# First attention round prepared inside the embedding stage: projection, rotation, K pages and V gathers between the embedded groups

## What is computed

```python
W = weights[condition]                                   # (64, 32, 32): one of 16 mixing matrices per sequence
y = einsum('bct,bcd->bdt', x, W)                         # mixes the 32 tokens
x = x + (y.astype(f16) @ dequantise(qweight, qzeros, scales) + bias)
# attention: 32 query heads, 8 key/value heads of width 128, 512 cached keys in 16 pages of 32, and 32 new keys
q, k, v = x @ Wq.T, x @ Wk.T, x @ Wv.T
q, k = rope(rmsnorm(q, q_norm_w), pos), rope(rmsnorm(k, k_norm_w), pos)   # pos = cache_seqlens + arange(32)
k_all, v_all = concat(k_cache[block_table], k), concat(v_cache[block_table], v)
out = softmax(mask(q @ k_all.T * SCALE)) @ v_all @ Wo.T
```

## Time and profile before

| | |
|---|---|
| median of 3 runs | 3275.6 us (3273.37 to 3278.69) |
| the profiled execution | 3281.08 us, span in the profile 3279.6 us |
| TensorE busy | 3045.8 us (93%), granted clock 0.971 on average |
| VectorE, ScalarE, POOL busy | 1544.9, 1289.2, 1557.0 us |
| DMA | 378.97 MB, mean 116 GB/s |
| first instruction of the embedded groups on TensorE | 36.53 us |
| attention block entered | 127.2 us |
| first scores of round 0 | 178.15 us |

### The profile page before, as it was taken

The page is one execution under the profiler, slowest core; times in us unless marked ns, Lnnn a source line. Parts: engine busy times, 40 slices in busy tenths (PEclk is TensorE's granted clock), DMA queues, the critical chain, the costliest instruction groups (busy, mean ns, idle before and its releaser), DMA issues. The chain is left out here.

```text
span 3279.6 us, 56025 instructions
## 1 busy us (share of the span) xinstructions
PE 3045.8 (93%) x15264; PEld 2027.5 (62%) x15264; DVE 1544.9 (47%) x3914; ACT 1289.2 (39%) x3015; POOL 1557.0 (47%) x1335
## 2 busy tenths in 40 slices
PE   3689999999999999999999999999999996888887
PEld 2356666666666666666666666666666663555454
DVE  4334444444444444444444444444444444556555
ACT  1244444444444444444444444444444431222121
POOL 8455555555555555555555555555555520000000
PEclk9889999999999999999999999999999997999898
DMA  6724444444444443535334444344444343112110
GB/s 220 261 59 131 121 127 123 123 117 123 123 121 122 119 119 116 193 116 167 116 116 119 125 122 122 117 119 120 120 125 127 117 156 104 31 37 50 34 30 13
DMA packets 416381, 378.97 MB, mean 116 GB/s; under 512 B 83460, under 2 KB 347796, under 8 KB 415157
## 3 DMA queue, kind: packets, MB, share of 16 engines
q1 hardware_dynamic: 364676, 200.64, 20.9%
q0 software_dynamic: 50640, 174.92, 17.1%
q10 hardware_dynamic: 864, 0.63, 0.1%
HBM read 341.75 MB, written 25.85 MB: 112 GB/s over the span
## 5 line engine op out<-in xcount | busy, mean ns | idle before, releaser
L537 DVE CUSTOM_DVE_ANT_0 ps_s<-ps_s,mask 128x544 f32<-128x544 f32 x512 | 375.0, 732 | 950.6 <-PE ps_s L360 798.8
L319 PE MATMUL ps_t<-wqkv,xT 128*128 128x512 f32 x1536 | 724.2, 595 | 7.1 <-DMA xT<-x1T_scratch 7.1
L212 POOL DMA_INDIRECT v_sb<-in_v_rows_w,v_row x512 | 497.3, 971 | 477.4 <-PE ps_oT L385 264.1
L383 PEld LDWEIGHTS ps_oT<-pT,v_sb 128*128 128x128 f32 x4096 | 528.0, 192 | 184.6 <-issue 183.9
L435 ACT ACTIVATE ps_s<-ps_s,nmax 128x544 f32<-128x544 f32 x512 | 352.3, 688 | 606.3 <-DVE nmax L537 518.3
L383 PE MATMUL ps_oT<-pT,v_sb 128*128 128x128 f32 x4096 | 542.5, 276 | 7.4 <-issue 7.3
L343 PE MATMUL ps_t<-wo,oT 128*128 128x512 f32 x1024 | 524.7, 596 | 3.5 <-ACT v_raw L430 1.4
L359 PE MATMUL ps_s<-k_sb,qT 128*128 128x416 f32 x1024 | 448.8, 520 | 15.2 <-issue 11.0
L547 DVE TENSOR_SCALAR p_sb<-ps_s,rinv 128x544 f32<-128x544 f32 x512 | 401.4, 784 | 23.5
L450 ACT ACTIVATE oT<-ps_oT 128x128 f32<-128x128 f32 x512 | 142.6, 278 | 656.4 <-PE ps_oT L385 610.1
L319 PEld LDWEIGHTS ps_t<-wqkv,xT 128*128 128x128 f32 x1536 | 264.5, 192 | 198.0 <-issue 190.7
(11 more groups left out here) (212 smaller groups left out, 3757.5 us busy)
## 6 DMA issues: line engine op xcount, KB each, us to landing
k_sb<-in_kT SPq DMA_DIRECT2D x2048, 64.0 KB
xT<-x1T_scratch POOLq DMA_DIRECT2D x32, 256.0 KB
tab<-rope_scratch POOLq DMA_DIRECT2D x32, 256.0 KB
v_sb<-in_v_rows_w,v_row POOLq DMA_INDIRECT x512
wo<-in_wo_w POOLq DMA_DIRECT2D x2, 4096.0 KB, 14.3
v_new<-v_raw SPq DMA_DIRECT2D x128, 64.0 KB, 1.9
y_scratch<-y_sb SPq DMA_DIRECT2D x32, 256.0 KB
wqkv<-in_wqkv_w SPq DMA_DIRECT2D x6, 1024.0 KB, 12.7
```

The source lines that it names most:

```text
L212: e.indirect_dma_start(out=v_sb[:, b % 2, c, :], out_offset=None, in_=A["v_rows_w"], in_offset=bass.IndirectOffsetOnAxis(ap=v_row[:, b, c: ...
L319: m = e.matmul(ps_t[bank_of(t)][:, :], xT[:, k, :], wqkv[:, k, 512 * t:512 * t + 512], start=k == 0, stop=k == KC - 1)
L383: e.matmul(ps_oT[:, :], v_sb[:, b % 2, c, h * D:(h + 1) * D], pT[:, u % 2, c, :], start=c == 0, stop=False)
L537: e.tensor_tensor_reduce(out=scores(u), in0=scores(u), in1=mask[:, b % 2, :], scale=-SCALE, scalar=3e38, op0=ALU.add, op1=ALU.min, accum_o ...
```

## The change

The tiles and semaphores that both stages need (`raw`, `rot`, `tab`, `xT`, `k_sb`, `v_sb`, ...) are made once, in a class `Shared` whose object `W` lives through both stages. `embed` places its short-lived tiles (packed weights, angles, sines, gathered mixing matrices) inside them. `rotate` becomes a function of the module; its text is the same. What changes in the order of work:

- The mixing matrices come in three parts (groups 0 to 3, 4 to 9, 10 to 15). TensorE waits only for the part that it needs.
- The angles are computed by VectorE, three of their steps as one fused instruction each, ahead of the dequantisation. The table with the minus sign is no longer computed: the norm weights are negated instead.
- The loads for the fold and all six loads of `wqkv` are issued by ScalarE, ahead of its first copy of a group. ScalarE also issues the stores of x1T.
- In groups 4 to 9 TensorE, ScalarE and VectorE also handle one projection tile of round 0 each. x1T of group 0 is written straight into `xT`.
- SP loads K pages of the first two sequences, four after each of groups 5 to 12.
- POOL makes the tables in two halves through one half-size buffer, takes those of group 0 by a copy, then issues the first eight V gathers and runs both rotations of round 0.
- The two sums of the fold are done by VectorE after groups 10 and 12. All 16 groups are written out, no loops.
- The load of the first half of `wo` is issued at the start of the attention, where TensorE now begins with `turn_q`.

```diff
@@ attention @@
-            e.dma_start(xT[:, :, :], x1T_d[0]).then_inc(dma_x, 16)
-            e.dma_start(tab[:, :, :], tab_d[0]).then_inc(dma_tab, 16)
...
-            load_v(0, 0)
-            load_v(0, 1)
+            load_x(1)
             e.dma_start(wo[:, :, :], A["wo_w"][0]).then_inc(dma_wo[0], 16)
-            rotate(0, 0)
-            rotate(0, 1)
-            e.wait_ge(raw_copied, NT)
-            load_x(1)
             body(0, 2)
...
-            for t in range(NT):
-                project(0, t, 0, KC)
             for t in range(NQT):
                 turn_q(0, t)
             score(0, 0, 0)
@@ embed @@
+    MIX_PARTS = [(0, 4), (4, 10), (10, GROUPS)]
+    SPREAD_AT = {1: 1, 5: 2}
+
+    FOLD_AT = 3
+    PROJECT_AT = {4: 0, 5: 1, 6: 2, 7: 3, 8: 4, 9: 5}
+    PAGES_AT = {5: (0, 0), 6: (0, 1), 7: (0, 2), 8: (0, 3), 9: (1, 0), 10: (1, 1), 11: (1, 2), 12: (1, 3)}
+    SUMS_AT = {10: ("w2f", "w2"), 12: ("b2f", "b2")}
...
+            # gpsimd
+            gather(0)
+            gather(1)
...
+            tables(0)
+            gather(2)
+            e.wait_ge(out_tab, 16)
+            tables(2)
...
+            e.wait_ge(deq, 1)
+            for b in range(2):
+                for c in range(LC):
+                    e.indirect_dma_start(out=W.v_sb[:, b, c, :], out_offset=None, in_=A["v_rows_w"],
+                                         in_offset=bass.IndirectOffsetOnAxis(ap=W.v_row[:, b, c:c + 1], axis=0)).then_inc(W.dma_v[b], 16)
...
+            rotate(e, W, 0, 0)
+            rotate(e, W, 0, 1)
...
+            # tensor
+            def project(t):
+
+                if t == 0:
+                    e.wait_ge(x1T_copied, 1)
+                    e.wait_ge(folded_a, 2)
+                e.wait_ge(dma_wqkv[t], 16)
+                wait(e, W.summed, t - 1)
+                for k in range(KC):
+                    m = e.matmul(ps_p[bank_of(t)][:, :], W.xT[:, k, :], wqkv[:, k, 512 * t:512 * t + 512], start=k == 0, stop=k == KC - 1)
+                m.then_inc(W.projected, 1)
...
+            # scalar
+            e.wait_ge(dma_q, 16 * 5)
+            for name in ("w2t", "b2t", "a13", "w2", "b2"):
+                e.dma_start(fold[name], A["c_" + name]).then_inc(dma_fold, 16)
+            e.wait_ge(ang_ready, 1)
+            e.activation(sn, ang, ACT.Sin).then_inc(trig, 1)
+            e.activation(cs, ang, ACT.Sin, scale=0.5).then_inc(trig, 1)
+            for t in range(NT):
+                at = slice(512 * t, 512 * t + 512)
+                e.dma_start(wqkv[:, :, at], A["wqkv_w"][0][:, :, at]).then_inc(dma_wqkv[t], 16)
...
+                wait(e, out_xT[g % 2], 16 * (g // 2))
+                e.activation(to, ps_x[g % 2][:, :, :], ACT.Copy).then_inc(x1T_copied, 1)
+                e.wait_ge(x1T_copied, g + 1)
+                e.dma_start(x1T_d[g], to).then_inc(out_xT[g % 2], 16)
```

More of the change, by code:

```diff
@@ L885, in body @@
[L885 removed]
+            spread(0)
+            e.wait_ge(W.dma_bt, 16)
+            e.tensor_scalar(W.bt[:, :], W.bt[:, :], 0, PAGES - 1, ALU.max, ALU.min).then_inc(W.bt_bounded, 1)
+            for g in range(GROUPS):
+                i = g % 2
                 e.wait_ge(ffn_done, g + 1)
```

486 lines of the change are left out of this document (251 added, 235 removed).

## The result

| | before | after |
|---|---|---|
| median, same chip | 3277.14 us (4 runs) | 3244.91 us (3236.72 to 3248.76, 4 runs) |
| profiled execution, its span | 3281.08, 3279.6 us | 3248.76, 3246.8 us |
| first mix on TensorE | 36.53 us | 39.88 us |
| attention entered | 127.2 us | 133.6 us |
| first scores of round 0 | 178.15 us | 143.50 us |

The ratio is 0.9897, with a 95% interval of 0.9885 to 0.991. The change gains 32 us where 53 were predicted, and the time lies above the range of 3207 to 3238. The first scores came at 143.5, not at 125: these 18.5 us are nearly all of the 20.8 us between the profiled execution and the 3228 predicted for it.

What follows compares the result with a forecast made beforehand. TensorE fills the rounds, so the first score's time decides. Lead-in -40.6 and earlier block entry -12.5 sum to -53 us: 3281.1 to 3228 for the profiled execution, 3222 for the median; range 3207 to 3238.

Steps and rivals of the forecast that it cites:

- Lead-in: From block entry to first scores of round 0: falls from 50.9 to 10.3 us, -40.6 us, leaving mainly `turn_q`.
- The rounds keep what the start gains: Rounds after the first are untouched, so what the first score gains, the whole gains: 53 us.
- rival D: Rounds stay at clock 0.94 instead of 1.00 after the denser start: 116 us slower, 3392; chance 0.03.
- Start of the groups: Before the first groups: angles on VectorE 7.5 us, first `mix` at 25 to 31 us instead of 36.5.
- The port cost: POOL's second tables blocking VectorE in groups 4 or 5: counted as 2 us, range 0 to 8.
- Standing in issue until about 32: ScalarE's queue at the start: issuing fold and `wqkv` loads delays its first copy to 32 us, range 26 to 40.
- The stall at group 2 to 3: Third x1T copy waits for a store queued behind eleven loads on ScalarE's queue, until 50 us.
- The fold's product on TensorE hides in this stall: At groups 2 to 3: the fold's product runs during the stall that lasts until 50 us, so it costs nothing extra.
- Groups 4 to 9: Each takes 2.51 us plus a projection tile of 3.81 us, 6.32 us; from 51 to 90 us.
- Groups 10 to 15: Late groups to last cast: 12.6 us plus 3 for fold sums, with pages and port conflicts; last cast at 107.6.
- Last cast to entry: End of the embedding to attention entry: 7.1 us as before, so the block is entered at 114.7 us.
- Rival B: Transfers or POOL set the end of the groups: gain 42 or 43 us, 3234 or 3233; chance 0.20.

Runs made afterwards that it cites:

- fold_first: Changed kernel with the fold's product and its copies moved ahead of the first mix on TensorE; 3230.91 us, ratio 0.9853.
- start_rebuilt: Changed kernel with the edits of tables_wait and fold_first, POOL waiting for each table product, and VectorE's fold sums after groups 2 and 3; 3231.08 us, ratio 0.9848.
- spread_first: Changed kernel with VectorE spreading the first part of the mixing matrices before the angles; 3234.55 us, ratio 0.9861.
- tables_wait: Changed kernel with the first spread between angles and dequantisation, and POOL's tables waiting for the dequantised weight; 3237.45 us, ratio 0.9865.
- same_again: Changed kernel run once more, unaltered; 3239.01 us, ratio 0.9871.

## Why the prediction was right and wrong

*Lead-in*, -40.6 us: right. From block entry at 133.64 to the first scores there are 9.9 us, against 10.3 predicted and 50.9 before. `turn_q` ran at 1.86 us a tile directly behind entry.

*The rounds keep what the start gains*: right on the whole. That 3103.3 and 3101.5 us agree within 2 us is luck in part, since other kernels with the same rounds took 3091.0 to 3109.6. The clock in the stretch from 290 on is 1.00 again, so rival D fell.

*Start of the groups*: "First `mix` at 25 to 31" came at 39.88. The angles (15.37 to 23.4, 8 us) cost what was said, 7.5. The failed terms are "the spread of four groups about a quarter of 4.32 us", which measured 8.08, and the last step of the dequantisation, 2.80 for 1.23 us. Both stand beside POOL's work on the tables, which starts as soon as ScalarE has its sines. The port cost was counted once, for the second tables, at 2 us of a range of 0 to 8. Measured are about 8.4 us at the first tables (6.8 and 1.6) and 8.4 at the second (9.13 for 0.69). This is the first step that failed: a cost put at nothing in one place and at 2 us in the other. The prediction had priced the whole run, 10 us, and took it for the upper end.

*"Standing in issue until about 32"*: the issues ended at 29.46, within the 26 to 40 given. But the first copy, set to 32 by it, came at 42.00, because it waited for TensorE.

*"The stall at group 2 to 3"*, until 50: wrong in mechanism, near in time. No copy waited for the x1T store. A transfer did hold TensorE until 53.90, but it was the x tile of group 4 on SP's queue, 18 us behind the last issue of the weights. That POOL's first table store filled the engines then fits the times, but was not tried. What held group 4 longer was VectorE's addition, to 61.68.

*"The fold's product on TensorE hides in this stall"*: wrong, the second step that failed. TensorE did stand idle, for 4.22 and 4.58 us, but both times ahead of the fold: in its order the fold comes behind the transpose of group 2, which needs the long addition. So the 8.1 us stand bare behind it; fold_first got 7.5 us back. Together the steps put the end of the fold at 70.7 where group 4 was to start at 51, 19.7 us late. Groups 4 to 9 won back 3.4 and groups 10 to 15 lost 2.7, which leaves 19.0 at the last cast and 18.5 at the first scores.

Repairs do not recover all of it: with both collisions and the fold out of the way start_rebuilt cast group 4 at 57.75, and the earliest first scores of any run are 131.04, not 125.

*Groups 4 to 9* at 6.32 us each: they took 5.63, a little better. *Groups 10 to 15* with pages and sums: 20.3 us against 17.6, with two waits for x tiles of 3.13 and 2.60 us in them. *Last cast to entry*, 7.1: measured 7.0. *POOL* ended its rotation near 120 instead of 102, before the block ended at 133.6, so off the path as said.

*Rival B*, transfers or POOL set the end: in the changed kernel only in small, by these two waits and the x tile at 53.90. It became the limit when the other losses were gone, and then through the pages on SP's queue, not as a sum of bytes at a rate.

The size of the gain was overstated because each mechanism that I could name was priced by its own row, and the one that the trace before showed clearly, 9.97 us for one addition, was discounted to 2.

## What to carry to other kernels

When two engines block each other, the same instruction can lose one instruction of the other engine or a whole run of them. So price the collision by the longest row of it, at every place where the moved work can meet the other engine, and not once. When work moves into a stage, look at what it makes earlier: a gain on one engine slides the loads behind it into the transfers of another queue, and single gains of 7 us need not add up. Before work is to hide in a stall, look on which side of the stall its place in the order is. Keep bulk loads off the queue of the load that the next step needs.

## What the runs showed of the hardware that was not expected

**VectorE can wait out a whole run of POOL products.** Beside four products of 2.3 us back to back one addition that takes 0.42 or 0.69 us alone took 9.97 (the kernel before), 9.13, 8.90, 8.98, 8.98 and 10.93 us in six kernels. In spread_first and tables_wait no addition beside such a run took more than 2.73 us, about one product. The four small copies lost about one product each, never a run. With a wait of POOL behind each product no addition beside the tables took more than 2.73.

**TensorE pauses where the hardware loop of the rounds returns, in some executions and not in others.** The timeline of TensorE in the changed kernel at such a place, and the table by stretch around it:

```profile
784.29 1.13 PE L359 MATMUL ps_s<-k_sb,qT 128*128 128x416 f32 x2 [2.03 <-issue]
783.00:789.00 6.00, 4.71 (x11) 2.43 (x12) 0.79 (x2) 1.06 (x4) 3.77 (x4) 0.72 0.68 201
```

It waits for nothing that the profile shows for 2.03 us, then some us at the lower clock (0.72 on average over these 6 us). At the same place of fold_first there is no pause:

```profile
782.65 0.86 PE L359 MATMUL ps_s<-k_sb,qT 128*128 128x416 f32 x2
```

Such pauses of over 0.5 us between 230 and 1300 us, about 159 us or a multiple of it apart, one turn of a loop of two rounds, were six in the changed kernel, five of them in this rhythm (10.4 us), two in same_again (4.2), none in fold_first, one in start_rebuilt (1.1). They go with the time from the first scores to the end. Of the sixteen profiled executions with the change, the six with under 2 us of pauses took 3091.0 to 3098.6 us, and the seven with 7 us or more took 3102.0 to 3109.6. This may be why one kernel's runs spread over 12 us (3236.72 to 3248.76) and a first score 5 us earlier need not show in the time. What decides the pauses stays open; whether the block before the rounds has a part in it was not tried.
